# Graph-network kernel, fourth layer: the segment sums of 512 edges formed at once instead of 128 edges at a time

## The chip, the cores and the metric

The kernel runs on one core of a Trainium2 chip. The metric is device time in microseconds (us) of one execution of the whole kernel. The core has five engines that run side by side, each in the order of its own instruction stream: PE (TensorE, matmuls), DVE (VectorE), ACT (ScalarE), POOL (GpSimd, which here issues the indirect DMAs) and SP (SyncE, which issues the plain DMAs). They wait for each other on semaphores only.

## The reference, cut to what matters

A node table `x` of 50000 rows and 128 columns passes through four graph layers over the same 25000 edges (`src`, `dst`, sorted by `dst`). The change bears on the sum over edges in the last layer:

```python
h = jnp.maximum(_layernorm(x, axis=-1), 0.0)
x = x + L3(h, edge_index, edge_weight, W, b, gamma, beta)
# in L3: self loops are appended to the edges, then
norm = dinv[row] * dinv[col] * ew
h = x @ W + b
msgs = norm[:, None] * h[row]
out = jax.ops.segment_sum(msgs, col, num_segments=n)
mean = jnp.mean(out, axis=0)
var = jnp.mean(jnp.square(out - mean), axis=0)
out = (out - mean) * jax.lax.rsqrt(var + BN_EPS) * gamma + beta
return jax.nn.relu(out)
```

The kernel sums the normalised rows first, before the product with `W`, and gathers their second moments for the batch norm at the same time.

## The kernel before, in words

The edges are padded to 25600, that is 200 tiles of 128 (`P`), taken in 50 groups (`NGE`) of four tiles (`G` = 4, 512 edges). One phase after the other works through the layers; the phases are separated by barriers. The first phase loads everything small: SP walks through a list `plan` of DMAs (L343 to L364, issued by the loop at L369) and PE and DVE begin only when all of them have landed (L478, L674). In the same phase DVE makes `firsts` (L729), which is 1 for each edge whose `dst` equals the one of the last edge of the tile in front; it is stored as `first_d`, and the later phases load it, 512 values per group, into one partition of the tile `carry` (`load_carry`, L212).

The phase that the change is about is the last one over edges (L1653 to L1854), called the edge phase below. For a group it does this:

- POOL gathers the four tiles of source rows into `xs` (`rows`, L1694) and, six steps later, scatters the four finished tiles of `rd` into the table `r_d` (`scatter`, L1700). Ahead of the gathers stands `written` (L1689), which waits for the scatters and for the moments of the group eight steps back. POOL's stream is unrolled.
- SP loads the destination rows into `rd`, a broadcast of the group's `dst` into `bc`, the links into `carry`, and a share of the node table into `nv`.
- DVE takes the row statistics (`stats`, L1745), makes scale and offset of the layer norm (`inverse`, `weigh`, `offset`), builds the masks (`sames`, L1766: for tile j, a 128 x 128 matrix that is the weight of edge p where edges p and e of that tile have the same `dst`), and adds the sums to the node's own part (`own`, L1774, which gives `v_ready`).
- ACT applies the norm and the relu to the 8 tiles of a group (`relus`, L1800, eight instructions, the last gives `h_ready`), takes the square root (`roots`), and copies the sums from PSUM to SBUF (`total`, L1794).
- PE forms the sums (`total`, L1820): for tile j one matmul with the mask of the tile, and one that adds, through `carry`, the last row of the sum of tile j-1. So tile j needs the copy by ACT of the sum of tile j-1. PE also accumulates the second moments of the finished rows (`moments`, L1833) and of the nodes (`node_moments`, L1844).

The order on each engine is set by `pipeline(eng, n, parts, slots)` (L66): in step k the engine runs the parts in the order of the list, each on group k minus its lag. The lists of the phase before are:

```python
pipeline(dve, NGE, [(inverse, 2), (weigh, 2), (own, 5), (weighed, 2), (offset, 2), (stats, 1), (sames, 2), (rows_summed, 1),
                    (differences, 1), (tails, 2), (squares, 1), (total, 1)], S8)
pipeline(act, NGE, [(total(0), 3), (total(1), 3), (relus, 2), (total(2), 3), (total(3), 3), (roots, 1)], S8)
pipeline(pe, NGE, [p for j in range(G) for p in ((total(j), 3), (moments(j), 7), (node_moments(j), 2, -1))], S8)
unrolled(NGE, [(written, S8), (rows, 0), (scatter, 6)], S8)      # POOL
```

An f32 matmul is two instructions in the trace, so the counts of PE rows are twice the number of matmuls in the code.

Of the kernel before, what the change touches and what calls it, by code (L numbers as in the profile page):

```python
# [16 lines left out]
F32 = mybir.dt.float32  # L17
BF16 = mybir.dt.bfloat16
F16 = mybir.dt.float16
I32 = mybir.dt.int32  # L20
# [104 lines left out]
def build(nc, t, debug):  # L125

    root = ExitStack()
    with root:
        def dram(name, shape):
            return nc.dram_tensor(name, shape, F32, kind="ExternalOutput" if debug else "Internal").ap()  # L130
# [7 lines left out]
        dst_d = dram("dst_d", (EP,))  # L138
        first_d = dram("first_d", (EP,))
        x2_d = dram("x2_d", (NN + EP, D))  # L140
        x3_d = dram("x3_d", (NN + EP, D))
# [5 lines left out]
        def sb(name, shape, dt=F32, ctx=root):  # L147
            return ctx.enter_context(nc.sbuf_tensor(f"{name}_{stage[0]}", shape, dt))
# [62 lines left out]

        def load_carry(eng, g, s):  # L212
            return eng.dma_start(carry[P - 1:P, s % 4, :, :].rearrange("a j e -> a (j e)"),
                                 first_d[bass.ds(g * (G * P), G * P)].rearrange("(a e) -> a e", a=1))

# [55 lines left out]
        with phase() as c:  # L271
# [9 lines left out]
            cnt = sb("cnt", [P, 1], F32, c)  # L281
            before = sb("before", [NT // 2, 2], I32, c)
            beforeF = sb("beforeF", [NT // 2, 2], F32, c)
            firsts = sb("firsts", [NT // 2, 2, P], F32, c)
            iota = sb("iota_b", [P, NLO], F16, c)
# [54 lines left out]
            def as_col(ap):  # L340
# [5 lines left out]
                     (before[1:NT // 2, 0:1], as_col(t["dst"][P - 1:(NT // 2) * P - 1:P])),  # L346
                     (before[0:1, 0:1], as_col(t["next_dst"][EP - 1:EP]))]
            plan += [(K[:, :], t["consts"][:, 0:K_COLS]), (K0[:, :], t["consts"][:, K_COLS:K_COLS + Z_COLS])]
            plan += [(rowsF[:, 3, :, :], t["edge_weight"].rearrange("(a r p) -> r a p", a=2, p=P))]
# [16 lines left out]
            with nc.Block() as block:  # L366
                @block.sync
                def _(sp):
# [5 lines left out]
                    sp.wait_ge(firsts_ready, 1)  # L374
                    sp.dma_start(first_d.rearrange("(a r p) -> r a p", a=2, p=P), firsts[:, :, :]).then_inc(rows_out, 16)
                    sp.wait_ge(groups_ready, 1)
                    n = groups_of_low(sp)
                    for s in range(2):
                        for conv in range(2):
                            sp.sem_inc(sums_out[conv][s], 16)  # L380
                    sp.wait_ge(rows_out, 48)

# [283 lines left out]
                def _(dve):  # L666
# [61 lines left out]
                    link(nc.vector.tensor_copy(beforeF[:, :], before[:, :]))  # L728
                    for k in range(2):  # L729
                        link(nc.vector.tensor_scalar(firsts[:, k, :], rowsF[:, 1, k, :], beforeF[:, k:k + 1], None, ALU.is_equal))  # L730
                    dve.sem_inc(firsts_ready, 1)
# [307 lines left out]
        with phase() as c:  # L1039
# [42 lines left out]
            with nc.Block() as block:  # L1082
# [21 lines left out]
                @block.sync  # L1104
                def _(sp):
                    def bc_used(g, s):
                        sp.wait_ge(same_ready, g + 1)

                    def load_bc(g, s):
                        sp.dma_start(bc[:, s % 4, :], dst_d[bass.ds(g * (G * P), G * P)].partition_broadcast(P)).then_inc(  # L1110
                            bc_in[s % 4], 16)

                    def first_used(g, s):
                        hold("sp", sp, sum_in, g * G + G + 1)

# [217 lines left out]
        with phase() as c:  # L1333
# [49 lines left out]
            with nc.Block() as block:  # L1383
# [18 lines left out]
                def _(sp):  # L1402
# [16 lines left out]
                    def load_first(g, s):  # L1419
                        load_carry(sp, g, s).then_inc(first_in[s % 4], 16)  # L1420

# [231 lines left out]
        with phase() as c:  # L1653
# [21 lines left out]
            first_in = [sem(f"gc_first_in{s}") for s in range(4)]  # L1675
            sum_p = bank[4]

# [6 lines left out]
            with nc.Block() as block:  # L1684
# [25 lines left out]
                def _(sp):  # L1710
# [11 lines left out]
                    def first_used(g, s):  # L1722
                        hold("sp", sp, sum_in, g * G + G + 1)

                    def load_first(g, s):
                        load_carry(sp, g, s).then_inc(first_in[s % 4], 16)

# [7 lines left out]
                def _(dve):  # L1735
# [3 lines left out]
                    nc.vector.memset(bank[1][:, :], 0.0).then_inc(gram_zero, 1)  # L1739
                    nc.vector.memset(sums[:, 3, G - 1, :], 0.0).then_inc(sum_in, 1)  # L1740
                    dve.wait_ge(sum_in, 1)
                    dve.sem_inc(set_up, 1)
# [47 lines left out]
                def _(act):  # L1790
                    act.preload_act_table(ACT.Sqrt)
                    act.wait_ge(set_up, 1)

                    def total(j):  # L1794
                        def part(g, s):
                            act.wait_ge(sum_ps, g * G + j + 1)
                            nc.scalar.activation(sums[:, s % 4, j, 0:D + 1], sum_p[:, 0:D + 1], ACT.Copy).then_inc(sum_in, 1)  # L1797
                        return part
# [10 lines left out]
                    roots = rooting(act, tmp, root, mixed, rooted)  # L1809
                    pipeline(act, NGE, [(total(0), 3), (total(1), 3), (relus, 2), (total(2), 3), (total(3), 3), (roots, 1)], S8)  # L1810

                @block.tensor
                def _(pe):
# [5 lines left out]

                    def total(j):  # L1820
                        def part(g, s):
                            if j == 0:
                                pe.wait_ge(same_ready, g + 1)
                                pe.wait_ge(h_ready, g + 1)
                                pe.wait_ge(first_in[s % 4], count4(g, s))
                            before = sums[:, s % 4, j - 1, 0:D + 1] if j else sums[:, (s - 1) % 4, G - 1, 0:D + 1]
                            pe.wait_ge(sum_in, g * G + j + 1)
                            nc.tensor.matmul(sum_p[:, 0:D + 1], same[:, s % 4, j, :], xs[:, s, j, 0:D + 1], start=True, stop=False)  # L1828
                            nc.tensor.matmul(sum_p[:, 0:D + 1], carry[:, s % 4, j, :], before, start=False,
                                             stop=True).then_inc(sum_ps, 1)  # L1830
                        return part

                    def moments(j):  # L1833
# [10 lines left out]
                    def node_moments(j):  # L1844
# [198 lines left out]
```

## Time and profile before

| what | us |
|---|---|
| median of 3 runs | 3221.45 |
| lowest and highest of them | 3214.99, 3222.52 |
| the profiled execution, its own time | 3215.13 |
| its span in the trace | 3213.3 |

| engine | busy us | share of the span |
|---|---|---|
| PE (matmul) | 2140.7 | 67% |
| DVE | 2130.8 | 66% |
| ACT | 1683.2 | 52% |
| POOL | 1601.0 | 50% |

The mean granted clock of TensorE is 0.825 of full speed over the span. Shares are means over phases with different limits, so the change has to be read from its own phase, which runs from about 2399 to 2920 us of the span. A row of a timeline gives the start, the duration, the engine, the line and operation, `out<-in`, the number of merged instructions and in square brackets the idle time of the engine before it with what ended it. In a view of waits, "issue" means that nothing in the profile explains the pause. The ends of matmuls are modelled: two in a row overlap in the record, so the rate of PE is read from starts.

### The profile page before, as it was taken

To read this page: it belongs to the slowest core of one execution; us is meant where nothing else is said; L and a number is where in the kernel's file an instruction comes from. 1 tells how busy PE (TensorE), PEld (TensorE's weight loads), DVE (VectorE), ACT (ScalarE), POOL (GpSimd) and SP (SyncE) were. 2 spreads that over 40 slices of the span, in tenths; PEclk is the share of its full clock that TensorE was granted. 3 is DMA by queue.
4 is the path that set the end of the run, shared out by engine and by line. 5 is a ranking of instruction groups with operands and counts; after the bars stand their busy time and mean duration, and the time that the engine had idled before them with its cause. 6 is when DMAs were issued, how large, how long until landed. Compare 5 with 4: busy or idle time off the path is not lost. (4 is left out here: it accounts for less than half of the span.)

```text
span 3213.3 us, 49191 instructions
## 1 busy us (share of the span) xinstructions
PE 2140.7 (67%) x10561; PEld 1506.1 (47%) x10561; DVE 2130.8 (66%) x8711; ACT 1683.2 (52%) x4589; POOL 1601.0 (50%) x1511
## 2 busy tenths in 40 slices
PE   3673333627775877877845787778866777773666
PEld 1232331425554766666632333334436666662555
DVE  5688323308885988888957777777726444451999
ACT  2493001217883666566646988898945444440222
POOL 3200556350005888888827655565507777774000
PEclk9797667869995777676767999998988887886999
DMA  2297323429998887787837999999966555542998
GB/s 68 87 371 318 63 34 75 128 33 291 323 324 268 250 246 243 243 248 245 247 91 216 288 291 288 284 294 281 278 167 201 181 185 184 183 151 90 305 325 284
DMA packets 494679, 696.61 MB, mean 217 GB/s; under 512 B 66363, under 2 KB 357398, under 8 KB 485932
## 3 DMA queue, kind: packets, MB, share of 16 engines
q1 hardware_dynamic: 416414, 511.30, 50.6%
q0 software_dynamic: 63360, 130.75, 15.2%
q10 hardware_dynamic: 14736, 52.96, 4.4%
q14 instruction: 143, 1.17, 0.1%
q8 instruction: 26, 0.43, 0.1%
HBM read 394.91 MB, written 327.18 MB: 225 GB/s over the span
## 5 line engine op out<-in xcount | busy, mean ns | idle before, releaser
L262 POOL DMA_INDIRECT xs<-x_d,table_src x400 | 384.5, 961 | 361.1 <-DVE x L1491 133.5
L262 POOL DMA_INDIRECT xs<-n_d,srcI x200 | 241.4, 1207 | 327.2 <-DVEq L1140 271.3
L262 POOL DMA_INDIRECT xd<-n_d,dstI x200 | 220.7, 1103 | 61.0 <-issue 53.6
L262 POOL DMA_INDIRECT xd<-x_d,table_dst x200 | 211.2, 1056 | 65.1 <-issue 64.8
L1705 POOL DMA_INDIRECT r_d<-rd,out_row x200 | 196.8, 984 | 61.5 <-issue 58.8
L1828 PE MATMUL bank<-xs,same 128*128 128x129 f32 x400 | 106.6, 356 | 129.3 <-DVE same L1770 64.9
L1646 PEld LDWEIGHTS bank<-nmsg,same 128*128 128x128 f32 x400 | 62.5, 196 | 265.6 <-ACT sums L1578 206.2
L1646 PE MATMUL bank<-nmsg,same 128*128 128x128 f32 x400 | 101.2, 336 | 126.8 <-ACT sums L1578 74.1
L457 POOL DMA_INDIRECT sum_d<-add,to x40 | 65.1, 1629 | 235.8 <-ACT add L654 225.4
L238 DVE RECIPROCAL rs<-root 128x4 f32<-128x4 f32 (+3 forms) x253 | 52.0, 205 | 188.1 <-ACT root L257 171.0
L257 ACT ACTIVATE root<-tmp,eps 128x4 f32<-128x4 f32 (+3 forms) x253 | 76.7, 303 | 189.4 <-DVE tmp L233 189.1
L1749 DVE BATCH_NORM_STATS2 st<-xs 128x6 f32<-128x128 f32 x200 | 43.5, 280 | 194.6 <-DMA xs<-x_d,table_src 194.6
L1030 PE MATMUL bank<-T,K 128*128 128x512 f32 x196 | 108.7, 636 | 91.5 <-DMA mt<-meta_d 90.7
L1019 ACT ACTIVATE T<-bank,nb,rs 128x128 f32<-128x128 f32 x392 | 147.3, 456 | 42.5 <-DVE nb L249 41.2
L1849 PE MATMUL bank<-nv 128*128 128x130 f32 x784 | 163.2, 340 | 5.2 <-DMA nv<-v_d 5.2
L1274 ACT ACTIVATE nt<-nt,nb,rs 128x128 f32<-128x128 f32 x392 | 160.2, 483 | 2.5 <-DVE nb L249 2.5
L1960 ACT ACTIVATE wT<-bank 128x512 f32<-128x512 f32 x98 | 58.5, 597 | 186.0 <-DVE y L1984 132.8
L1594 ACT ACTIVATE nv<-nx,nb,rs 128x128 f32<-128x128 f32 x392 | 155.9, 489 | 0.0
L555 PE MATMUL bank<-across,reach 128*128 128x129 f32 x160 | 48.2, 398 | 159.4 <-ACT he L646 118.3
L1264 ACT ACTIVATE xd<-xd,nb,rs 128x128 f32<-128x128 f32 x200 | 82.4, 482 | 123.9 <-DVE nb L249 123.9
L531 PE MATMUL bank<-mask,h 128*128 128x512 f32 x160 | 91.3, 724 | 80.8 <-DVE mask L862 55.5
L1828 PEld LDWEIGHTS bank<-xs,same 128*128 128x128 f32 x400 | 75.8, 236 | 147.7 <-ACT sums L1797 73.1
(383 smaller groups left out, 7294.3 us busy)
## 6 DMA issues: line engine op xcount, KB each, us to landing
n_d<-T SPq DMA_DIRECT2D x98, 528.0 KB, 3.7
nt<-n_d SPq DMA_DIRECT2D x49, 1056.0 KB, 7.2
r<-r_d SPq DMA_DIRECT2D x98, 520.0 KB, 5.5
bc<-dst_d SPq DMA_DIRECT2D x170, 256.0 KB, 4.7
r_d<-nv SPq DMA_DIRECT2D x49, 528.0 KB, 8.0
v_d<-nv SPq DMA_DIRECT2D x49, 528.0 KB, 7.7
nv<-v_d SPq DMA_DIRECT2D x49, 528.0 KB, 4.1
x_d<-x SPq DMA_DIRECT2D x100, 256.0 KB, 4.2
```

The costliest lines, as they stand in the source:

```text
L257: nc.scalar.activation(root[:, s, :], tmp[:, s % 2, 2, :], ACT.Sqrt, bias=eps[:, :], scale=1.0 / D).then_inc(rooted, 1)
L262: pool.indirect_dma_start(out=out, out_offset=None, in_=table, in_offset=bass.IndirectOffsetOnAxis(ap=index, axis=0)).then_inc(s, 16)
L531: last = nc.tensor.matmul(group_sums[s][:, :], h[:, s, k, :], mask[:, s, k, :], start=k == 0, stop=k == G - 1)
L1019: last = nc.scalar.activation(T[:, s, j, 0:D], bank[s][:, j * P:(j + 1) * P], ACT.Relu, bias=nb[:, s, j:j + 1], scale=rs[:, s, j:j + 1])
L1030: nc.tensor.matmul(bank[s][:, :], ident, T[:, s, :, HW:XW], start=True, stop=False, skip_group_check=True)
L1264: last = nc.scalar.activation(hd[:, s, j, :], hd[:, s, j, :], ACT.Identity, bias=nb[:, at, B + j:B + j + 1], scale=rs[:, at, B + j:B + j + 1])
L1274: last = nc.scalar.activation(nt[:, s % 4, j, 0:D], nt[:, s % 4, j, 0:D], ACT.Identity, bias=nb[:, s, j:j + 1], scale=rs[:, s, j:j + 1])
L1594: last = nc.scalar.activation(nv[:, s % 4, j, 0:D], nx[:, s % 4, j, :], ACT.Relu, bias=nb[:, at, C3 + j:C3 + j + 1], scale=rs[:, at, C3 + ...
L1646: nc.tensor.matmul(sum_p[:, 0:D], same[:, s % 2, j, :], nmsg[:, s % 2, j, :], start=True, stop=False)
L1705: pool.indirect_dma_start(out=r_d, out_offset=bass.IndirectOffsetOnAxis(ap=out_row[:, edges:edges + 1], axis=0), in_=rd[:, s, j, :], in_of ...
L1828: nc.tensor.matmul(sum_p[:, 0:D + 1], same[:, s % 4, j, :], xs[:, s, j, 0:D + 1], start=True, stop=False)
L1849: last = nc.tensor.matmul(bank[7][:, 0:D + 2], nv[:, s % 4, i, 0:D], nv[:, s % 4, i, 0:D + 2], start=False, stop=False, skip_group_check=True)
```

## The change

In the edge phase the mask of tile k now spans the edges from tile k to the end of the group (512, 384, 256, 128 columns), and the sum of tile j is the total of the matmuls of masks 0 to j (ten in a group instead of four). One link per group is left: four matmuls with `carry` all add the last row of the group in front. A second table of links, `group_first_d`, is made for it in the first phase: an edge counts there if its `dst` equals that of the last edge of the group in front. The sums stand in four PSUM banks, two per group by turns, and ACT copies them in two halves. PE issues the four links of a group as `linked`, at the end of its step; ACT's list has both copies first, then `relus`. The two other phases with the old sums keep them.

```diff
@@ first phase @@
-            before = sb("before", [NT // 2, 2], I32, c)
-            firsts = sb("firsts", [NT // 2, 2, P], F32, c)
+            before = sb("before", [NT // 2, 4], I32, c)
+            firsts = sb("firsts", [NT // 2, 4, P], F32, c)
...
+            for r in range(G):
+                plan += [(before[r:NT // 2:G, 3:4], as_col(t["dst"][(NT // 2) * P - 1:EP - 1:G * P])),
+                         (before[G + r:NT // 2:G, 2:3], as_col(t["dst"][G * P - 1:(NT // 2) * P - 1:G * P])),
+                         (before[r:r + 1, 2:3], as_col(t["next_dst"][EP - 1:EP]))]
...
-                    sp.dma_start(first_d.rearrange("(a r p) -> r a p", a=2, p=P), firsts[:, :, :]).then_inc(rows_out, 16)
+                    sp.dma_start(first_d.rearrange("(a r p) -> r a p", a=2, p=P), firsts[:, 0:2, :]).then_inc(rows_out, 16)
+                    sp.dma_start(group_first_d.rearrange("(a r p) -> r a p", a=2, p=P), firsts[:, 2:4, :]).then_inc(rows_out, 16)
...
-                    for k in range(2):
-                        link(nc.vector.tensor_scalar(firsts[:, k, :], rowsF[:, 1, k, :], beforeF[:, k:k + 1], None, ALU.is_equal))
+                    for k in range(4):
+                        link(nc.vector.tensor_scalar(firsts[:, k, :], rowsF[:, 1, k % 2, :], beforeF[:, k:k + 1], None, ALU.is_equal))
@@ edge phase @@
-            same = sb("same", [P, 4, G, P], F32, c)
+            same = sb("same", [P, 4, G, G * P], F32, c)
...
-            sum_p = bank[4]
+            sum_p = [[bank[2], bank[3]], [bank[5], bank[6]]]
...
-                        hold("sp", sp, sum_in, g * G + G + 1)
+                        hold("sp", sp, sum_in, g * 2 + 4)
...
-                        load_carry(sp, g, s).then_inc(first_in[s % 4], 16)
+                        load_carry(sp, g, s, group_first_d).then_inc(first_in[s % 4], 16)
...
-                            to = bc[:, s % 4, j * P:(j + 1) * P]
-                            last = nc.vector.tensor_scalar(same[:, s % 4, j, :], to, dstF[:, bass.ds(g * G + (j + 1), 1)],
+                            to = bc[:, s % 4, j * P:]
+                            last = nc.vector.tensor_scalar(same[:, s % 4, j, j * P:], to, dstF[:, bass.ds(g * G + (j + 1), 1)],
                                                            w_src[:, bass.ds(g * G + j, 1)], ALU.is_equal, ALU.mult)
...
-                        dve.wait_ge(sum_in, g * G + G + 1)
+                        dve.wait_ge(sum_in, g * 2 + 4)
@@ ACT @@
-                    def total(j):
+                    def total(half):
                         def part(g, s):
-                            act.wait_ge(sum_ps, g * G + j + 1)
-                            nc.scalar.activation(sums[:, s % 4, j, 0:D + 1], sum_p[:, 0:D + 1], ACT.Copy).then_inc(sum_in, 1)
+                            act.wait_ge(sum_ps, g * 2 + 2 - half)
+                            nc.scalar.activation(sums[:, s % 4, 2 * half:2 * half + 2, :], sum_p[s % 2][half][:, 0:2 * TW].rearrange(
+                                "p (j f) -> p j f", j=2), ACT.Copy).then_inc(sum_in, 1)
                         return part
...
-                    pipeline(act, NGE, [(total(0), 3), (total(1), 3), (relus, 2), (total(2), 3), (total(3), 3), (roots, 1)], S8)
+                    pipeline(act, NGE, [(total(1), 3), (total(0), 3), (relus, 2), (roots, 1)], S8)
@@ PE @@
-                    def total(j):
+                    def in_group(j):
                         def part(g, s):
-                            if j == 0:
+                            if j == G - 1:
                                 pe.wait_ge(same_ready, g + 1)
                                 pe.wait_ge(h_ready, g + 1)
-                                pe.wait_ge(first_in[s % 4], count4(g, s))
-                            before = sums[:, s % 4, j - 1, 0:D + 1] if j else sums[:, (s - 1) % 4, G - 1, 0:D + 1]
-                            pe.wait_ge(sum_in, g * G + j + 1)
-                            nc.tensor.matmul(sum_p[:, 0:D + 1], same[:, s % 4, j, :], xs[:, s, j, 0:D + 1], start=True, stop=False)
-                            nc.tensor.matmul(sum_p[:, 0:D + 1], carry[:, s % 4, j, :], before, start=False,
-                                             stop=True).then_inc(sum_ps, 1)
+                            for k in range(j + 1):
+                                nc.tensor.matmul(sum_of(s, j), same[:, s % 4, k, j * P:(j + 1) * P], xs[:, s, k, 0:D + 1], start=k == 0 and j % 2 == 1,
+                                                 stop=False, skip_group_check=True)
                         return part
+
+                    def linked(g, s):
+                        pe.wait_ge(first_in[s % 4], count4(g, s))
+                        pe.wait_ge(sum_in, g * 2 + 1)
+                        before = sums[:, (s - 1) % 4, G - 1, 0:D + 1]
+                        for half in (1, 0):
+                            for j in (2 * half + 1, 2 * half):
+                                last = nc.tensor.matmul(sum_of(s, j), carry[:, s % 4, j, :], before, start=False, stop=True,
+                                                        skip_group_check=True)
+                            last.then_inc(sum_ps, 1)
...
-                    pipeline(pe, NGE, [p for j in range(G) for p in ((total(j), 3), (moments(j), 7), (node_moments(j), 2, -1))], S8)
+                    pipeline(pe, NGE, [p for j in (3, 2, 1, 0) for p in ((in_group(j), 3), (moments(3 - j), 7), (node_moments(3 - j), 2, -1))] +
+                             [(linked, 3)], S8)
```

## Rows read from the trace of the kernel before

**Rows 1.** Windows of the edge phase and its neighbours.

```profile
core 0: us, PE busy (x) PEld busy (x) DVE busy (x) ACT busy (x) POOL busy (x), PEclk, DMA share, GB/s
2600.00:2700.00 100.00, 74.53 (x480) 63.35 (x479) 47.10 (x240) 44.29 (x130) 76.06 (x79) 0.83 0.53 184
```

**Rows 2.** Groups of instructions, window 2388 to 2925.

```profile
L1705 POOL DMA_INDIRECT r_d<-rd,out_row x200 | 196.8, 984 | 61.5 <-issue 58.8 <-DMA r_d<-rd,out_row 1.2 <-PE bank L1839 1.2
L262 POOL DMA_INDIRECT xs<-x_d,table_src x200 | 193.4, 967 | 139.8 <-DVEq L1742 74.8 <-issue 50.3 <-DMA r_d<-rd,out_row 9.1
...
L1779 DVE SCALAR_TENSOR_TENSOR rd<-sums,rg_dst,rd 128x129 f32<-128x129 f32 x200 | 58.0, 351 | 12.8 <-ACT sums L1797 9.5 <-issue 0.8
```

**Rows 3.** Waits in the steady stretch, 2440 to 2895: total, times, longest.

```profile
PE bank L1828 <- ACT sums L1797: 58.5, 41, 4.2
PE bank L1828 <- DVE same L1770: 55.6, 37, 4.2
POOL xs L262 <- PE bank L1839: 4.7, 1, 4.7
```

**Rows 4.** Timeline of PE at full clock, tile after tile in one step.

```profile
2620.72 0.39 PE L1828 MATMUL bank<-xs,same 128*128 128x129 f32 x2
2620.94 0.39 PE L1829 MATMUL bank<-sums,carry 128*128 128x129 f32 x2
2621.17 0.39 PE L1838 MATMUL bank<-rd 128*128 128x130 f32 x2
...
2621.61 0.71 PE L1849 MATMUL bank<-nv 128*128 128x130 f32 x4
...
2622.16 0.39 PE L1828 MATMUL bank<-xs,same 128*128 128x129 f32 x2
```

**Rows 5.** Timeline of ACT and PE from the relus of a group on.

```profile
2449.70 1.64 ACT L1803 ACTIVATE xs<-xs,nb,rs 128x128 f32<-128x128 f32 x4
...
2452.78 0.26 ACT L1797 ACTIVATE sums<-bank 128x129 f32<-128x129 f32 x1
2453.10 0.49 PE L1828 MATMUL bank<-xs,same 128*128 128x129 f32 x2 [1.18 <-ACT sums L1797]
2453.42 0.39 PE L1829 MATMUL bank<-sums,carry 128*128 128x129 f32 x2
2453.85 0.28 ACT L1797 ACTIVATE sums<-bank 128x129 f32<-128x129 f32 x1 [0.80 <-PE bank L1829]
```

**Rows 6.** Groups of instructions by form, whole span: wider copies and masks.

```profile
L1960 ACT ACTIVATE wT<-bank 128x512 f32<-128x512 f32 x98 | 58.5, 597 | 186.0 <-DVE y L1984 132.8
L890 DVE TENSOR_SCALAR combine<-bcs,srcF,low 128x512 f32<-128x512 f32 x20 | 11.2, 558 | 12.4 <-PE bank L567 10.9 <-DMA bcs<-src_d 1.5
L1770 DVE TENSOR_SCALAR same<-bc,dstF,w_src 128x128 f32<-128x128 f32 x200 | 56.0, 357 | 0.0
```

**Rows 7.** Windows around PE's first sums, and with PE hardly pausing; columns as in rows 1.

```profile
2415.00:2420.00 5.00, 2.28 (x10) 2.28 (x11) 4.52 (x25) 2.77 (x8) 3.78 (x5) 0.50 0.43 107
...
2460.00:2465.00 5.00, 4.72 (x39) 4.25 (x40) 3.15 (x15) 2.08 (x9) 3.78 (x5) 1.00 0.42 133
```

**Rows 8.** Timeline: first sums on PE, and the last scatter on POOL.

```profile
2417.72 0.80 PE L1828 MATMUL bank<-xs,same 128*128 128x129 f32 x2 [9.32 <-DVE same L1770]
...
2916.16 0.97 POOL L1705 DMA_INDIRECT r_d<-rd,out_row  x1 [0.30 <-issue]
```

**Rows 9.** Timeline of the first phase: loads on SP's queue, and the first work.

```profile
2.02 0.77 SPq L370 DMA_DIRECT2D before<-dst  x2
2.83 0.26 SPq L370 DMA_DIRECT2D before<-next_dst  x1
...
17.69 0.43 SPq L370 DMA_DIRECT2D r_b<-L_gnn_b  x1
22.86 0.56 DVE L675 CAST rowsF<-rows 100x768 f32<-100x768 int32 x1 [22.86 <-DMA r_b<-L_gnn_b]
...
47.62 0.87 DVE L812 BATCH_NORM_STATS2 st<-er 128x6 f32<-128x128 f32 x4 [2.92 <-DMA er<-x,ix]
```

More of the change, by code:

```diff
@@ L139, in build @@
         first_d = dram("first_d", (EP,))
+        group_first_d = dram("group_first_d", (EP,))
         x2_d = dram("x2_d", (NN + EP, D))
@@ L209, in node_rows_of, with load_carry @@
             return table[bass.ds(g * (G * P), G * P), 0:width].rearrange("(p j) f -> p j f", p=P)
-        def load_carry(eng, g, s):
+        def load_carry(eng, g, s, table):
             return eng.dma_start(carry[P - 1:P, s % 4, :, :].rearrange("a j e -> a (j e)"),
-                                 first_d[bass.ds(g * (G * P), G * P)].rearrange("(a e) -> a e", a=1))
+                                 table[bass.ds(g * (G * P), G * P)].rearrange("(a e) -> a e", a=1))
         def equal_rows(out, to, g):
@@ L281, in build @@
             cnt = sb("cnt", [P, 1], F32, c)
-            before = sb("before", [NT // 2, 2], I32, c)
-            beforeF = sb("beforeF", [NT // 2, 2], F32, c)
-            firsts = sb("firsts", [NT // 2, 2, P], F32, c)
+            before = sb("before", [NT // 2, 4], I32, c)
+            beforeF = sb("beforeF", [NT // 2, 4], F32, c)
+            firsts = sb("firsts", [NT // 2, 4, P], F32, c)
             iota = sb("iota_b", [P, NLO], F16, c)
@@ L380, in _ @@
                             sp.sem_inc(sums_out[conv][s], 16)
-                    sp.wait_ge(rows_out, 48)
+                    sp.wait_ge(rows_out, 64)
                     def stages(conv):
@@ L1116, in load_first @@
                     def load_first(g, s):
-                        load_carry(sp, g, s).then_inc(first_in[s % 4], 16)
+                        load_carry(sp, g, s, first_d).then_inc(first_in[s % 4], 16)
                     def store(g, s):
@@ L1419, in load_first @@
                     def load_first(g, s):
-                        load_carry(sp, g, s).then_inc(first_in[s % 4], 16)
+                        load_carry(sp, g, s, first_d).then_inc(first_in[s % 4], 16)
                     def store(g, s):
@@ L1722, in first_used @@
                     def first_used(g, s):
-                        hold("sp", sp, sum_in, g * G + G + 1)
+                        hold("sp", sp, sum_in, g * 2 + 4)
                     def load_first(g, s):
-                        load_carry(sp, g, s).then_inc(first_in[s % 4], 16)
+                        load_carry(sp, g, s, group_first_d).then_inc(first_in[s % 4], 16)
                     def load_nodes(g, s):
@@ L1739, in _ @@
                     nc.vector.memset(bank[1][:, :], 0.0).then_inc(gram_zero, 1)
-                    nc.vector.memset(sums[:, 3, G - 1, :], 0.0).then_inc(sum_in, 1)
-                    dve.wait_ge(sum_in, 1)
+                    nc.vector.memset(sums[:, 3, G - 1, :], 0.0).then_inc(sum_in, 2)
+                    dve.wait_ge(sum_in, 2)
                     dve.sem_inc(set_up, 1)
@@ L1818, in _, with sum_of @@
                                      skip_group_check=True)
-                    def total(j):
+                    def sum_of(s, j):
+                        return sum_p[s % 2][j // 2][:, (j % 2) * TW:(j % 2) * TW + D + 1]
+                    def in_group(j):
                         def part(g, s):
-                            if j == 0:
+                            if j == G - 1:
                                 pe.wait_ge(same_ready, g + 1)
                                 pe.wait_ge(h_ready, g + 1)
-                                pe.wait_ge(first_in[s % 4], count4(g, s))
-                            before = sums[:, s % 4, j - 1, 0:D + 1] if j else sums[:, (s - 1) % 4, G - 1, 0:D + 1]
-                            pe.wait_ge(sum_in, g * G + j + 1)
-                            nc.tensor.matmul(sum_p[:, 0:D + 1], same[:, s % 4, j, :], xs[:, s, j, 0:D + 1], start=True, stop=False)
-                            nc.tensor.matmul(sum_p[:, 0:D + 1], carry[:, s % 4, j, :], before, start=False,
-                                             stop=True).then_inc(sum_ps, 1)
-                        return part
+                            for k in range(j + 1):
+                                nc.tensor.matmul(sum_of(s, j), same[:, s % 4, k, j * P:(j + 1) * P], xs[:, s, k, 0:D + 1], start=k == 0 and j % 2 == 1,
+                                                 stop=False, skip_group_check=True)
+                        return part
+                    def linked(g, s):
[7 more added lines that the diff above has]
+                            last.then_inc(sum_ps, 1)
                     def moments(j):
```

## The prediction

> **What bounds the phase now.** I read the windows first. In the edge phase no engine is full: of 100 us PE is busy 74.5, POOL 76.1, DVE 47.1, ACT 44.3 [rows 1]. POOL's 76 is a full engine all the same. The groups of instructions give 0.967 us for a gather and 0.984 us for a scatter, each with a pause of about 0.31 us in front that is put down to "issue" or costs no more than that (61.5 us over 200 scatters) [rows 2]. Eight of them make 4 x (0.967 + 0.984) + 8 x 0.31 = 10.3 us per group; I use 10.25. In the view of waits POOL waited for real work for 4.7 us, once, early, for PE [rows 3]. So POOL's descriptor work paces the phase and the others fit in.
>
> PE fits in with little to spare. At full clock a tile takes from 2620.72 to 2622.16, 1.43 us: an f32 matmul of 129 or 130 columns advances by 0.22 us, the moments of one tile by 0.44, the two node matmuls by 0.55 with the gap behind them [rows 4]. A step of four tiles is 5.72 us. PE's waits for ACT's copies and for masks are 58.5 + 55.6 us over 455 us [rows 3], that is over 44.4 steps, 2.6 us each; so PE is at work for 7.7 of 10.25 us, and does 5.72 us of full-speed work in them: an effective clock of 0.745 of full. The granted clock explains that: it has two levels, 2.4 and 1.2 GHz, 0.83 in the mean here [rows 1]; it was 1.2 GHz while PE began its first sums after 9.3 us without work, and 2.4 GHz throughout where PE was busy 4.72 of 5 us [rows 7, 8].
>
> **The change, part by part.**
>
> *PE's work.* Eight matmuls for the sums become ten and four. Six more at 0.22 us add 1.32 us: a step is 7.04 us at full clock. The work would still fit under 10.25 us: 9.45 us at the effective clock of 0.745.
>
> *The order, which decides.* Before, ACT in a step copies two tiles of sums, does the relus of the next group, and copies the other two; the relus run beside PE's second and third tile. After, both copies stand ahead of the relus, and the second copy needs `linked`, which is the last thing in PE's step. PE's next step begins with `in_group(3)`, which waits for `h_ready`, the end of those same relus. Follow one group g: PE's step g+2 ends with the links of g-1; ACT's step g+2 copies g-1, then makes the relus of g; only then PE's step g+3 can start, and behind that first wait stand all of its moments and node matmuls, since it is in order. So a period is PE's whole step plus ACT's handover, and nothing of the one lies beside the other.
>
> *The handover.* The last link starts; ACT's copy begins 0.43 us later (2453.42 to 2453.85) [rows 5]. A copy of 264 columns lies between 0.28 us for 129 [rows 5] and 0.60 us for 512 [rows 6]; its next instruction can start about 0.1 us before its end, and I take 0.3 us, from the nearer row. The first half's copy runs beside the last two links. The eight relus take 3.1 us until ACT's next start (2449.70 to 2452.78) and about 0.1 more until the result; PE starts 0.06 us after ACT's end [rows 5]. Together 0.43 + 0.3 + 3.2 + 0.06 = 4.0 us, less the 0.22 us in which PE would still be issuing that link: PE stands for 3.75 us in every step.
>
> *The period.* 7.04 + 3.75 = 10.8 us even if PE always had its full clock, more than POOL's 10.25. At the effective clock of 0.745 it is 9.45 + 3.75 = 13.2 us. The pause is one of 3.75 us where there were two or so with 2.6 us in all, and PE works longer between two of them; these pull in opposite directions, so I keep 0.745 as the likeliest. Its ends: 0.90 (T = 11.6) if the longer bursts help more, 0.65 (T = 14.6) if the longer pause hurts more.
>
> *The sum.* The phase is now set by PE from its first sums at 2417.7 us [rows 8] to its last ones, then by the last copy, `own` and the last scatters.
> - 50 steps of 13.2 us: 660.
> - less the moments missing in the first four (4 x 0.44 / 0.745 each): 9.4; less the node matmuls missing in the last two (4 x 0.55 / 0.745 each): 5.9; less the last handover: 3.75. Left: 641.
> - wider masks ahead of the first step: a mask of 512 columns takes 0.558 us, one of 128 takes 0.357 [rows 6]; the four in between come to 1.83 instead of 1.43 us: 0.4, once. In the other steps DVE waits for rows anyway (it is under half busy, [rows 1]).
> - behind the last link: 0.8 us for the copy, 4 x 0.351 for `own` [rows 2], 4 x 1.28 for the scatters: 7.3.
> - end: 2417.7 + 0.4 + 641 + 7.3 = 3066.4. Before, the last scatter ended at 2917.1 [rows 8]. The phase grows by 149 us.
> The other extra work hides: two wider copies for four, the masks, and POOL, which now waits for PE in `written`.
>
> *The first phase.* SP issues twelve more small DMAs into `plan`, and PE and DVE wait for all (22.9 us) [rows 9]. The nearest rows are 0.30 us for a single value (0.26 and the 0.04 between entries) and 0.4 us for 100 values (2.02 to 2.83, two) [rows 9]; new are four of one and eight of 25 values. Bounds 3.6 and 4.9 us; I take 4.0, in full on the path, as SP issues its list without a pause up to 17.7 us. The two more `firsts` and one more store, at most 2 x 0.357 + 0.4 = 1.1 us, lie ahead of a wait of 2.9 us of DVE for gathered rows [rows 9]; taken as 0, and 1.1 if that cover is gone.
>
> Total: 149 + 4 = 153 us. The profiled execution took 3215.1 us, so 3368. It lies 6 us under the median of its three runs; I add half of that: **3371 us**. A measurement of this kernel can tell about 0.3%, 10 us, from no change.
>
> **The rivals.**
>
> *A. PE keeps its full clock.* Longer bursts end the half-speed stretches, T = 10.8. For it: 1.00 in the window with few pauses [rows 7]. Against: a pause of 3.75 us comes in every step, longer than most of today's, and today's already cost a quarter of the speed. By the same sum the phase ends near 2950, +33 us: 3255 us. An effective clock of 0.90 gives 3292. Chance 0.10.
>
> *B. PE is mostly at half speed.* Every burst starts at 1.2 GHz and leaves it late. Always at 1.2 GHz: T = 17.8, 3595 us; at 0.65 it is 3438. For it: the level after the long pause at the start [rows 7]. Against: the stretch at 1.00 shows that PE rises again under steady work, and the bursts are over 7 us. Chance for worse than 0.65: 0.08. The Trainium skill, "TensorE: Matmul & The Clock Gate", section "HAM oscillation — how this bites in real kernels", tells of a kernel whose waits between bursts were long enough that every burst started throttled. By that rule, if half the work of each burst went at 1.2 GHz (my estimate; an effective clock of 0.67), the time would be about 3425 us, inside the range; the trace agrees as far as its first burst began at 1.2 GHz.
>
> *C. POOL still sets the pace, not slower.* The loop closes between PE's last link and its next first matmul, but it only costs if it exceeds 10.25 us. It has 10.8 us at full clock; if a long run of matmuls went at 0.20 instead of 0.22 us (26 of them, 0.5 us) and the clock stayed full, the loop would just fit and the phase would end as before: only the 4 us of the first phase would remain, 3222 us. Both would have to hold, and the first wait of POOL at the start might even shrink. Chance 0.06 for within 0.3%.
>
> *D. A gain.* It needs POOL's wait of 4.7 us [rows 3] gone and a cover for the first phase; at most 1 to 2 us net. I leave 0.02 for what I don't see.
>
> The middle case, an effective clock from 0.65 to 0.90, keeps 0.74, and gives 3292 to 3438 us. That alone leaves out more than 2 in 10, so the range reaches down over most of A: **3260 to 3440**. Left out are B, C, D and a little of A, in all under 0.2. Slower by over 0.3%: 0.74 + 0.10 + 0.08 = 0.92; within: 0.06; faster: 0.02.
>
> **What the changed profile should show.** (1) The edge phase ends near 3066 us instead of 2917, and later phases keep their lengths. (2) POOL's issues no longer follow each other at 1.28 us: it waits some 3 us per group for PE (moments) or for DVE's `own`. (3) PE's wait ahead of `in_group` is put down to ACT's second half of the relus, some 3.6 us, about 50 times, and the waits for masks are gone. (4) ACT's copy waits for the links for most of PE's step. (5) The granted clock in the phase is between 0.65 and 0.85. (6) Matmuls of masks: 1000 rows, links: 400, copies: 100. (7) The first DVE work starts near 27 us. I am wrong in the main step if PE finds `h_ready` set when it comes to a new group, or if POOL is still back to back.

## The result and the profile after

The changed kernel takes 3406.5 us (median of 4 runs, 3401.7 to 3418.6) against 3218.2 us: ratio 1.059, 95% interval 1.057 to 1.061. It is slower by 188 us. The forecast was 3371 us in a range of 3260 to 3440.

The profiled execution took 3409.8 us with a span of 3408.0 us, 194.7 us more than before. The edge phase, from PE's first sums to the end of the last scatter, ran from 2433.5 to 3110.4 us: 676.9 us instead of 499.4, so 177.5 us of the growth are there. Its first sums come 15.8 us later than before; 8.5 us of that are the first phase (31.4 instead of 22.9 us to the first work), the rest is in phases that weren't edited. What follows the last scatter took 1.4 us more.

Windows of the edge phase (columns as in rows 1):

```profile
2600.00:2800.00 200.00, 149.03 (x897) 133.97 (x895) 77.84 (x372) 56.95 (x155) 116.21 (x117) 0.75 0.39 136
```

PE is as busy as before (74.5%, [rows 1]) while POOL, DVE and ACT all fell, POOL from 76 to 58%: nothing but PE's own loop is near its limit, and PE reaches that share with a clock of 0.75 instead of 0.83. The waits, 2450 to 3030 us:

```profile
ACT sums L1803 <- PE bank L1846: 401.6, 43, 9.8
DVE rs L239 <- ACT root L258: 340.1, 43, 8.5
PEld bank L1836 <- issue: 163.5, 43, 3.8
PE bank L1836 <- ACT rd L1813: 156.6, 43, 3.6
POOL xs L263 <- PE bank L1856: 143.2, 39, 12.2
```

Against rows 3: PE no longer waits for masks or for copies of sums, but 43 times, once per step, for the second half of the relus (L1813), 3.64 us each (156.6 / 43). ACT waits for the links nearly the whole of PE's step. POOL waits for PE's moments, where it had waited once. The chain can be followed in the timeline of one period:

```profile
2703.39 1.06 PE L1846 MATMUL bank<-sums,carry 128*128 128x129 f32 x8
2703.85 0.99 POOL L263 DMA_INDIRECT xs<-x_d,table_src  x1 [3.37 <-PE bank L1856]
2704.04 0.84 ACT L1803 ACTIVATE sums<-bank 128x264 f32<-128x264 f32 x2 [9.56 <-PE bank L1846]
2704.78 1.64 ACT L1810 ACTIVATE xs<-xs,nb,rs 128x128 f32<-128x128 f32 x4
...
2706.31 1.64 ACT L1813 ACTIVATE rd<-rd,nb,rs 128x128 f32<-128x128 f32 x4
...
2708.09 2.06 PE L1836 MATMUL bank<-xs,same 128*128 128x129 f32 x8 [3.64 <-ACT rd L1813]
...
2717.05 1.06 PE L1846 MATMUL bank<-sums,carry 128*128 128x129 f32 x8
...
2721.74 2.06 PE L1836 MATMUL bank<-xs,same 128*128 128x129 f32 x8 [3.64 <-ACT rd L1813]
```

Links, copy, eight relus, PE's first masks; then PE's step until the next links. The four links are issued within 4 x 0.22 us from 2703.39 on, so PE stands from 2704.27 to 2708.09, 3.82 us, and is at work for the other 9.83 us of a period of 13.65 us (2708.09 to 2721.74). The work is 7.04 us at full clock, so the effective clock is 7.04 / 9.83 = 0.72. Where the half-speed stretch lies shows in short windows of the same period:

```profile
2703.00:2706.00 3.00, 1.45 (x12) 1.26 (x12) 0.00 (x0) 1.90 (x6) 1.21 (x2) 1.00 0.07 22
2706.00:2709.00 3.00, 0.91 (x4) 0.94 (x5) 0.60 (x3) 2.14 (x7) 2.39 (x3) 0.71 0.74 260
2709.00:2712.00 3.00, 3.00 (x16) 2.73 (x15) 3.00 (x15) 0.00 (x0) 2.22 (x3) 0.50 0.57 206
2712.00:2715.00 3.00, 3.00 (x20) 2.73 (x19) 1.62 (x10) 0.00 (x0) 2.12 (x2) 0.65 0.25 89
```

The clock is full (2.4 GHz) when PE stops, falls to 1.2 GHz during the pause and stays there for the first part of the next burst. With two levels, a mean of 0.71 from 2706 to 2709 puts the fall near 2707.3, and 0.65 from 2712 to 2715 puts the rise near 2714.1: PE does the first 6.0 of its 9.8 us at work at half speed. Of the groups of instructions, those that answer to rows 2 and 6:

```profile
L1836 PE MATMUL bank<-xs,same 128*128 128x129 f32 x1000 | 227.1, 384 | 188.7 <-ACT rd L1813 178.4 <-DVE same L1776 10.3
L1711 POOL DMA_INDIRECT r_d<-rd,out_row x200 | 206.1, 1031 | 91.7 <-issue 59.1 <-PE bank L1856 25.8 <-DVE rd L1785 6.4
L263 POOL DMA_INDIRECT xs<-x_d,table_src x200 | 191.8, 959 | 278.5 <-PE bank L1856 150.6 <-DVEq L1748 73.6 <-issue 54.3
L1803 ACT ACTIVATE sums<-bank 128x264 f32<-128x264 f32 x100 | 39.0, 390 | 462.9 <-PE bank L1846 460.1
L1776 DVE TENSOR_SCALAR same<-bc,dstF,w_src 128x512 f32<-128x512 f32 x50 | 26.6, 533 | 0.0
```

And the first phase (compare rows 9):

```profile
2.02 0.77 SPq L375 DMA_DIRECT2D before<-dst  x2
2.83 0.26 SPq L375 DMA_DIRECT2D before<-next_dst  x1
3.14 1.72 SPq L375 DMA_DIRECT2D before<-dst  x2
...
5.36 1.51 SPq L375 DMA_DIRECT2D before<-dst  x2
6.91 0.41 SPq L375 DMA_DIRECT2D before<-next_dst  x1
...
31.42 0.56 DVE L681 CAST rowsF<-rows 100x768 f32<-100x768 int32 x1 [31.42 <-DMA r_b<-L_gnn_b]
```

The new DMAs of 25 values (24 in every second one) into every fourth partition take SP 0.71 to 0.76 us each, the first two 0.90 and 0.79, where one of 100 values into adjacent partitions takes 0.34 to 0.39 us. The new ones of a single value take 0.41 us, the old one 0.26.

### The profile page after: what moved, and what is told of

It is laid out like the page before. It is cut to its first block and busy times, and to the rows that moved or that the text cites. A ratio compares the mean times of both kernels' runs of the same rounds, so it can differ in the third digit from the quotient of the medians.

```text
span 3408.0 us, 50106 instructions
## 1 busy us (share of the span) xinstructions
PE 2269.7 (67%) x11161; PEld 1635.6 (48%) x11161; DVE 2148.7 (63%) x8713; ACT 1666.2 (49%) x4489; POOL 1614.0 (47%) x1511
## 5 line engine op out<-in xcount | busy, mean ns | idle before, releaser
L1836 PE MATMUL bank<-xs,same 128*128 128x129 f32 x1000 | 227.1, 384 | 188.7 <-ACT rd L1813 178.4
L1836 PEld LDWEIGHTS bank<-xs,same 128*128 128x128 f32 x1000 | 200.7, 289 | 197.1 <-issue 186.3
L1803 ACT ACTIVATE sums<-bank 128x264 f32<-128x264 f32 x100 | 39.0, 390 | 462.9 <-PE bank L1846 460.1
L1711 POOL DMA_INDIRECT r_d<-rd,out_row x200 | 206.1, 1031 | 91.7 <-issue 59.1
L1866 PE MATMUL bank<-nv 128*128 128x130 f32 x784 | 173.7, 356 | 4.3 <-DMA nv<-v_d 4.3
L1316 PE MATMUL bank<-xs,same 128*128 128x129 f32 x400 | 121.7, 398 | 30.8 <-ACT sums L1259 20.0
```

What stands on the lines that cost most here:

```text
L1711: pool.indirect_dma_start(out=r_d, out_offset=bass.IndirectOffsetOnAxis(ap=out_row[:, edges:edges + 1], axis=0), in_=rd[:, s, j, :], in_of ...
L1836: nc.tensor.matmul(sum_of(s, j), same[:, s % 4, k, j * P:(j + 1) * P], xs[:, s, k, 0:D + 1], start=k == 0 and j % 2 == 1, stop=False, skip ...
L1866: last = nc.tensor.matmul(bank[7][:, 0:D + 2], nv[:, s % 4, i, 0:D], nv[:, s % 4, i, 0:D + 2], start=False, stop=False, skip_group_check=True)
```

## The experiments

Two theories were set against each other: **loop** (PE's step and ACT's handover follow each other because of the order in which they are issued) and **work** (six more matmuls and wide masks are more than the engines can do in POOL's 10.25 us).

### The relus ahead of the copies

```diff
-                    pipeline(act, NGE, [(total(1), 3), (total(0), 3), (relus, 2), (roots, 1)], S8)
+                    pipeline(act, NGE, [(relus, 2), (total(1), 3), (total(0), 3), (roots, 1)], S8)
```

> The changed kernel with one edit: in ACT's list of the edge phase relus stands ahead of both copies, so the relus of group g no longer wait for the links of group g-1. All fourteen matmuls, the wide masks and the first phase stay. Theory 'loop' (PE's step and ACT's handover follow each other, 9.8 + 3.85 us): the loop is open, POOL paces again at 10.25 us per group, the edge phase from first sums to last scatter is 500 to 515 us instead of 677, and the kernel takes 3220 to 3245 us. Rival 'work' (six more matmuls and wider masks are too much for PE or DVE): the period stays near 13 us and the kernel at 3380 to 3410 us.

Measured: 3233.3 us, ratio to before 1.004 (1.002 to 1.006). The edge phase took 500.0 us (2432.7 to 2932.7), what it took before the change. Moving one entry of a list takes back 173 of the 188 us with all the work still done, which settles **work**. The waits, 2450 to 2900 us, look like rows 3 again (PE waits for masks, and for the relus only three times), and the windows show PE with more to do and still paced:

```profile
PE bank L1836 <- DVE same L1776: 85.8, 34, 4.6
PE bank L1836 <- ACT rd L1813: 3.1, 3, 1.3
POOL r_d L1711 <- issue: 53.0, 174, 0.3
```

```profile
2600.00:2700.00 100.00, 79.21 (x576) 70.97 (x576) 53.20 (x250) 41.26 (x109) 76.28 (x78) 0.90 0.51 177
```

### The links ahead of the moments

```diff
-                    pipeline(pe, NGE, [p for j in (3, 2, 1, 0) for p in ((in_group(j), 3), (moments(3 - j), 7), (node_moments(3 - j), 2, -1))] +
-                             [(linked, 3)], S8)
+                    pipeline(pe, NGE, [(in_group(j), 3) for j in (3, 2, 1, 0)] + [(linked, 3)] +
+                             [p for j in range(G) for p in ((moments(j), 7), (node_moments(j), 2, -1))], S8)
```

> The changed kernel with another edit: PE issues in_group(3) to in_group(0), then linked, and the moments and node moments of the step behind them; ACT's list is left as changed. Theory 'loop': the loop still closes through ACT, but moments and node matmuls (4 us at full clock) now lie beside the handover of 3.85 us, so the loop is 3.1 + 3.9 = about 7 us at full clock and under POOL's 10.25 us; the kernel takes 3220 to 3250 us. Rival 'work': near 3400 us, as the work is the same. If only the pause and its effect on the clock mattered, this and the version with the relus first should come out alike.

Measured: 3241.3 us, 1.007 (1.004 to 1.009). ACT's order is as in the change and the dependence is the same; it is only covered by work that doesn't hang on it. The edge phase took 505.4 us (2442.2 to 2947.6), 5.4 us more than with the relus first. The intervals of the two ratios overlap, so which of the two ways is better isn't shown.

### The pause filled with work that nobody needs

```diff
+                    def filler(g, s):
+                        for _ in range(12):
+                            nc.tensor.matmul(bank[4][:, 0:D], ident, ones, start=True, stop=True)
...
-                             [(linked, 3)], S8)
+                             [(linked, 3), (filler, 3)], S8)
```

> The changed kernel with twelve more f32 matmuls of 128 columns per step, into an unused bank, behind the links (2.6 us at full clock, 5.2 at half). They add nothing that is used. Theory 'loop with the clock': the period of 13.65 us holds 9.8 us of PE time for 7.04 us of full-speed work, because the pause drops the clock each time; with the pause filled the clock stays at full, the period is 7.04 + 3.85 = 10.9 us and the kernel 3265 to 3300 us, faster by 110 to 140 us with more work. Rival 'the clock is not moved by the pause': the period stays 13.65 or grows, and the kernel takes 3400 us or more. Rival 'work': 12 x 0.22 us x 50 = 130 us more, 3540 us.

Measured: 3275.6 us, 1.019 (1.016 to 1.022): 131 us faster than the change, with 600 more matmuls. The edge phase took 549.8 us (2425.2 to 2975.0), 127 us less than in the change. The period was 10.96 us, and the granted clock didn't leave its upper level:

```profile
2700.00:2800.00 100.00, 91.35 (x771) 84.26 (x770) 47.46 (x225) 37.72 (x104) 71.92 (x74) 1.00 0.49 169
```

```profile
2699.87 2.84 PE L1874 MATMUL bank<-K 128*128 128x128 f32 x24
2703.68 1.13 PE L1836 MATMUL bank<-xs,same 128*128 128x129 f32 x8 [0.96 <-ACT rd L1813]
```

The loop stays (7.04 + 3.82 = 10.9 us), but the part of the loss that the clock made is gone. So the 13.65 us are 10.25 us of POOL, 0.7 us by which the loop exceeds it at full clock, and 2.7 us for the half-speed stretch after each pause: of the 3.4 us lost in each step, four fifths are the clock's.

### The old sums with the relus last

```diff
-                    pipeline(act, NGE, [(total(0), 3), (total(1), 3), (relus, 2), (total(2), 3), (total(3), 3), (roots, 1)], S8)
+                    pipeline(act, NGE, [(total(0), 3), (total(1), 3), (total(2), 3), (total(3), 3), (relus, 2), (roots, 1)], S8)
```

> The kernel before with one edit: in ACT's list of the edge phase relus stands behind all four copies, as in the change, and the sums stay as they were. Theory 'loop': the period is PE's step (5.72 us at full clock) and the part of the handover that nothing covers; here the moments and node matmuls of the last tile (1.0 us) lie beside it, so the pause is about 2.7 us, and the loop 8.4 us at full clock, 10.3 at the effective clock of 0.745: hardly over POOL's 10.25, so 3220 to 3260 us. Rival 'the place of the relus in ACT's list is the whole cost': as slow as the change, 3380 us or more.

Measured: 3221.7 us, 1.003 (1.001 to 1.005); the edge phase 510.2 us (2413.9 to 2924.1). The place of the relus alone costs about 10 us of the phase, and nearly all of them once, at the start, and not in each step. There POOL waits twice, 13.5 us in all, where it had waited 4.7:

```profile
2434.87 1.00 POOL L1705 DMA_INDIRECT r_d<-rd,out_row  x1 [3.56 <-DVE rd L1779]
2459.87 0.98 POOL L262 DMA_INDIRECT xs<-x_d,table_src  x1 [9.95 <-PE bank L1839]
```

After that PE's period is 10.13 us, just under POOL's 10.25. With the old sums the loop also closes, but moments and node matmuls of the last tile stand behind the last link and cover a part; in the change nothing does. PE's pause is 2.6 us in each step (2.7 were expected):

```profile
PE bank L1828 <- issue: 100.5, 39, 2.6
```

The view puts most of it to issue. That it is the wait for the relus is argued from the timeline, where PE starts 0.2 us after their end.

### The new order with the old amount of matmuls

```diff
-                            for k in range(j + 1):
-                                nc.tensor.matmul(sum_of(s, j), same[:, s % 4, k, j * P:(j + 1) * P], xs[:, s, k, 0:D + 1], start=k == 0 and j % 2 == 1,
-                                                 stop=False, skip_group_check=True)
+                            nc.tensor.matmul(sum_of(s, j), same[:, s % 4, j, j * P:(j + 1) * P], xs[:, s, j, 0:D + 1], start=j % 2 == 1,
+                                             stop=False, skip_group_check=True)
```

> The changed kernel with one matmul per tile for the sums instead of one to four; the sums over earlier tiles of a group are left out. Order, links, masks and copies as changed. It has PE's old amount of work (5.72 us at full clock) in the new order. Theory 'loop': 5.72 / 0.72 + 3.85 = 11.8 us a period, edge phase about 590 us from first sums to last scatter, kernel 3310 to 3340 us: about half of the loss stays with no extra matmul. Rival 'work': POOL paces again, 3225 to 3240 us.

Measured: 3308.7 us, 1.029 (1.026 to 1.032), 1.3 us below the range that was expected; the phase took 581.9 us (2436.9 to 3018.7), mean period 11.6 us. PE's wait is the same as in the change, 3.64 us in each step (2450 to 2900 us):

```profile
PE bank L1835 <- ACT rd L1813: 142.0, 39, 3.6
```

The new order (the links at the end of PE's step, the relus last on ACT) costs some 80 us of the phase with no matmul added. The six matmuls add the other 95 us of the phase, but only because they lie inside the closed loop: in the version with the relus first they cost nothing that shows. At full clock this loop would take 5.72 + 3.82 = 9.5 us, an estimate from the steps above, and that is less than POOL's 10.25. By it the 80 us are there only because of the half-speed stretches.

### Four more matmuls inside the loop

```diff
+                    def more(g, s):
+                        for _ in range(4):
+                            nc.tensor.matmul(bank[4][:, 0:D], ident, ones, start=True, stop=True)
...
-                             [(linked, 3)], S8)
+                             [(more, 3), (linked, 3)], S8)
```

> The changed kernel with four more f32 matmuls of 128 columns per step into an unused bank, ahead of the links, so that they delay the copies. They add nothing that is used. The changed kernel's period is 13.65 us to 0.01 us from step to step, which hints that the clock's changes hold it to a fixed value. Theory 'held': the period stays 13.65 us and the kernel 3400 to 3415 us, although PE has 0.88 us more full-speed work in every step; the share of the time at full clock rises. Rival 'effective clock of 0.72 throughout': 0.88 / 0.72 = 1.2 us more in each step, 3460 to 3475 us.

Measured: 3415.7 us, 1.062 (1.059 to 1.065), 0.7 us above the range of the theory that the period is held, and 9 us over the change where 54 to 69 were expected by the constant effective clock. The edge phase took 681.4 us, 4.5 more than in the change. The mean period stayed 13.65 us, but it wasn't held from step to step: single periods went 13.3, 13.4, 14.3 us in turn. The pauses are as before (3.6 us), and the clock gives back what the matmuls take:

```profile
2600.00:2800.00 200.00, 145.39 (x994) 132.05 (x994) 73.80 (x356) 60.64 (x165) 114.72 (x118) 0.84 0.41 136
```

0.84 instead of 0.75. In the change 48 of 50 bursts of PE start at 1.2 GHz; here, from the eleventh on, only every third does. In this kernel the period of the loop is thus not proportional to its work: 11.6, 13.65 and again 13.65 us for 5.72, 7.04 and 7.92 us of full-speed work. Why it keeps the same mean isn't shown.

### The first phase by itself

The kernel before with all edits of the first phase and no other; then the same with `group_first_d` declared behind `r_d`; then the kernel before with the table alone:

```diff
         first_d = dram("first_d", (EP,))
+        group_first_d = dram("group_first_d", (EP,))
...
+                    sp.dma_start(group_first_d.rearrange("(a r p) -> r a p", a=2, p=P), firsts[:, :, :]).then_inc(rows_out, 16)
...
-                    sp.wait_ge(rows_out, 48)
+                    sp.wait_ge(rows_out, 64)
```

> The kernel before with only the edits of the first phase: four columns in before, twelve more DMAs in plan, four firsts and the table group_first_d, which is stored and not read. The edge phase is as before. The trace of the change shows the first work at 31.4 us instead of 22.9, so the first phase should cost 8 to 9 us: 3225 to 3230 us. In the profiled execution of the change the later, unedited attention phase was 13 us longer (645 instead of 632 us from its first to its last sums). If that comes from the shifted addresses or from the later start, it shows here too and the kernel takes 3238 to 3243 us; if it was variation between executions, it doesn't.

> The kernel before with the edits of the first phase as in e5_first_phase_only, but group_first_d declared behind all other tables, so that x2_d, x3_d, v_d and r_d keep their addresses. e5 cost 21 us, of which the first phase explains 8 to 9. Theory 'addresses': the rest goes, 3226 to 3229 us. Rival 'later start or variation': it stays, 3236 to 3243 us.

> The kernel before with nothing but the second table: group_first_d declared between first_d and x2_d, and one store of firsts into it (0.3 us of issue, 100 KB). Theory 'addresses': about 10 us slower than before (3223 to 3230 us), as e5 was about 13 us slower than the same kernel with the table declared last. Rival 'no effect of addresses; the difference of e5 and e7 was variation, and the rest beyond the first phase's 8.5 us comes with the later start': within 2 us of before.

Measured: 1.007 (1.005 to 1.009), that is 21 us; 1.004 (1.002 to 1.005), 12 us; and 1.000 (0.999 to 1.002), 1 us. The first two start their work at 31.0 and 31.8 us, so 8 to 9 us are the twelve DMAs. The second, 3226.5 us, lies in the range that the theory of addresses gave. But the two ran in different rounds, in which the kernel before took 3218.7 and 3213.1 us: the 13 us between them are 9 by their ratios, and the intervals of these overlap. The table alone, in its place, costs nothing where the theory wanted 10 us, and so it falls. What the first version lost beyond the first phase isn't explained. The unedited attention phase takes 632 to 646 us from its first to its last sums in the profiled executions of all these kernels (632.2 before, 645.5 after the change, 640.9 and 641.1 in these two, 639.2 with the table alone), with one profile of each. Whether the later start has a part in it stays open: the version with the filled pause also started at 31.1 us, and its attention phase took only 635.4.

### The change mended

The relus first as above, `group_first_d` declared last, and three DMAs for twelve:

```diff
-            for r in range(G):
-                plan += [(before[r:NT // 2:G, 3:4], as_col(t["dst"][(NT // 2) * P - 1:EP - 1:G * P])),
-                         (before[G + r:NT // 2:G, 2:3], as_col(t["dst"][G * P - 1:(NT // 2) * P - 1:G * P])),
-                         (before[r:r + 1, 2:3], as_col(t["next_dst"][EP - 1:EP]))]
+            def four_times(ap, n):
+                return ap.rearrange("(g a) -> g a", a=1).to_broadcast([n, G])
+            plan += [(before[0:NT // 2, 3:4], four_times(t["dst"][(NT // 2) * P - 1:EP - 1:G * P], NT // 2 // G)),
+                     (before[G:NT // 2, 2:3], four_times(t["dst"][G * P - 1:(NT // 2) * P - 1:G * P], NT // 2 // G - 1)),
+                     (before[0:G, 2:3], four_times(t["next_dst"][EP - 1:EP], 1))]
```

> The candidate for the best form of the change: relus first in ACT's list, the twelve DMAs of the first phase made with three (each value read four times through a source pattern that repeats it), and group_first_d declared last. The trace of the change shows 0.77 us per strided DMA on SP's queue against 0.39 for 100 adjacent partitions. Expected: first work at 24 to 25 us instead of 31.4, edge phase as before (500 us), kernel 3216 to 3224 us, no faster than the kernel before, since POOL still paces. Rival 'the freed engines give a gain': below 3208 us.

Measured: 3227.3 us, 1.002 (1.000 to 1.004), 3 us above the range that was expected; first work at 25.5 us (24 to 25 were expected), edge phase 498.5 us (2426.3 to 2924.8). SP's queue in its first phase:

```profile
3.13 1.84 SPq L376 DMA_DIRECT2D before<-dst  x2
5.02 0.64 SPq L376 DMA_DIRECT2D before<-next_dst  x1
25.49 0.56 DVE L682 CAST rowsF<-rows 100x768 f32<-100x768 int32 x1 [25.49 <-DMA r_b<-L_gnn_b]
```

It is no faster than the kernel before. No version beat the kernel before: with the loop open POOL's issuing of gathers and scatters paces the phase, and nothing in the change touches that.

## Why the prediction was right, point by point

- **POOL paced the phase** [rows 2, 3]. Shown by the mended versions: with PE's work up by nearly a quarter (7.04 for 5.72 us), the phase takes 500 us as before.
- **The closed loop.** Shown three ways: by moving the relus, by moving the links, and by keeping the order with the old work. PE's wait is put down to the second half of the relus once per step, as forecast, and the waits for masks are gone.
- **The handover, 3.75 us.** Measured 3.82. The copy of 264 columns took 0.39 us, inside its bounds.
- **The period, 13.2 us.** Measured 13.65 in the steady stretch. The term that was too small is the effective clock: 0.745 was taken, 0.72 measured. The prediction let the longer bursts and the longer pause cancel; the pause won. The first four periods ran at 10.3 to 10.8 us, so the mean over 49 is 13.4. Up to the start of the last group's masks PE needed 655.1 us where the sum gave 634.5 (641 less the last burst): 20.5 us of the miss. So the term of the sum that was mis-sized most is the 13.2 us of the period.
- **The end.** Taken: the last group's burst, its copy, `own` and four scatters, 13.8 us. Measured 21.8 from the start of that burst. Twelve scatters were left and not four: POOL's `written` stands ahead of them in its stream and waits for moments (5.82 us for L1856 ahead of the scatter at 3095.4), so those of three groups went one after the other. 8 us, and the step that failed is that only the last group's scatters were looked at.

```profile
3095.40 0.96 POOL L1711 DMA_INDIRECT r_d<-rd,out_row  x1 [5.82 <-PE bank L1856]
3109.42 0.97 POOL L1711 DMA_INDIRECT r_d<-rd,out_row  x1 [0.30 <-issue]
```

- **The first phase, 4.0 us.** Measured 8.5, outside the bounds of 3.6 and 4.9. They came from DMAs into adjacent partitions; the new ones took up to twice as long with a quarter of the values. So the number of values doesn't set SP's time. What does isn't shown: the new ones step by four partitions, and they also read every 512th value instead of every 128th. The three of the mended change write adjacent partitions, and those of 100 and 96 values took 0.95 and 0.85 us.
- **Phases between.** Forecast to keep their lengths; together 7 us longer, cause open (above), and those behind the edge phase 1.4 us.
- **The sum of the misses.** 20.5 + 8 + 4.5 + 7.3 + 1.4 = 41.7 us, which is what the profiled 3409.8 us lie above the 3368 of the sum. All have the same sign, so none hid another.
- **Rival A**, PE at full clock, had the price nearly right: its period of 10.8 us is the 10.96 us of the filled pause. Its 3255 us are 21 short of the 3276 measured there: 9 us in the periods, 9 at the end and 3.5 by the later start. Its condition wasn't met by the change itself. **Rival B** came in its mechanism and not in its price: 48 of the 50 bursts do start at 1.2 GHz and stay there for 6.0 of 9.8 us in the period shown. That gives the effective clock of 0.72 and not one under 0.65, as the clock rises within the burst. **Rival C**, POOL sets the pace, came true only once the loop was opened.

## What to carry to other kernels

When work is regrouped in a software pipeline, write down for each engine the order of its list and follow one group round: a result issued last in one engine's step, taken first in the other's, and ahead there of what the first engine waits for at the start of its next step, makes two steps that used to overlap a sum. The cure is an order in which each engine first does what the other waits for; here it cost nothing that shows. Whether a closed loop hurts depends on its length: with the old sums it was 10.13 us, under POOL's 10.25, and cost nothing per step. Ask before that what the regrouping can gain: here the sums were not what the phase waited for.

## What the runs showed that was not expected

- A pause of 3.8 us per step cost PE more by its clock (2.7 us of 13.65) than by being over POOL's pace (0.7 us), so 600 useless matmuls made the kernel 131 us faster.
- The period of the closed loop settled on 13.65 us, to 0.01 us from step to step after the first ten in the change, and kept that mean when each step got 0.88 us more full-speed work; with 1.32 us less it fell to 11.6. It also started at 10.4 us and went over to 13.65 when the moments joined.
- Issue times on SP's queue: 0.34 to 0.39 us for 100 single values into adjacent partitions, 0.71 to 0.90 us for 25 into every fourth, 0.95 us for 100 where the source pattern repeats each of 25 values four times.
